# All scores of an image in one stage on eight 32x64 tiles, in a shifted-window attention block on one Trainium2 core

## What is computed

```python
h = ln(x) * g1 + b1                              # over the 64 channels
h = roll(h, (-4, -4)); win = partition(h, 8)     # 16 windows of 64 positions per image
q, k, v = split(win @ qkv_w + qkv_b)             # 4 heads of 16 channels
attn = q @ k.T * 16 ** -0.5 + bias(rpb) + mask   # 64 x 64 per window and head
out = softmax(attn) @ v @ proj_w + proj_b
x = x + unroll(out)
x = x + gelu(ln2(x) @ fc1_w + fc1_b) @ fc2_w + fc2_b
```

## Time and profile before

| what | value |
|---|---|
| time of the program, median of 3 | 505.39 us (505.28 to 506.8) |
| time of the profiled execution | 505.93 us |
| its span, first to last instruction | 504.1 us |
| busy: PE, PEld, DVE, ACT, POOL | 461.7, 351.5, 380.6, 294.8, 379.5 us |
| mean granted TensorE clock | 0.989 of full speed |

### The profile page before, as it was taken

One profiled execution on the slowest core, in us unless ns is written; L12 is line 12 of the kernel. 1 busy time (PEld: TensorE's weight loads), 2 busy tenths in 40 slices (PEclk: granted clock), 3 DMA queues, 4 the chain that ended last, 5 costly groups with the idle time before them and its releaser, 6 DMA issues.

```text
span 504.1 us, 21443 instructions
## 1 busy us (share of the span) xinstructions
PE 461.7 (92%) x9630; PEld 351.5 (70%) x9630; DVE 380.6 (75%) x549; ACT 294.8 (58%) x437; POOL 379.5 (75%) x376
## 2 busy tenths in 40 slices
PE   0766999999999999999999999996999999999995
PEld 0534877877877887887887877785566766667664
DVE  2765897898898888889889889793477667776652
ACT  1234567647656556566566665534666777667761
POOL 2658989979979979979979888840588888888830
PEclk9997999999999999999999999999899999999999
DMA  8201442411411411511110110100002311320333
GB/s 164 63 1 33 118 98 53 107 25 41 110 25 34 117 25 29 123 25 28 40 25 23 44 25 24 44 4 3 1 19 71 85 42 46 85 72 18 85 90 81
DMA packets 9986, 27.04 MB, mean 54 GB/s; under 512 B 3368, under 2 KB 3368, under 8 KB 7976
## 3 DMA queue, kind: packets, MB, share of 16 engines
q1 hardware_dynamic: 9896, 25.68, 21.4%
HBM read 9.15 MB, written 8.39 MB: 35 GB/s over the span
## 4 chain that ended last, share of the span: by engine, by line
PE 80%; ACT 9%; DMA 4%; DVE 3%; SPq 1%; issue 1%; ACTq 0%; DVEq 0%
PE work L686 27%; PE outs L686 18%; PE scores L686 13%; PE trans L686 8%; PE trans L782 6%; ACT kT L603 4%; PE scores L822 4%; PE work L701 3%; ACT qT L605 3%; DMA params<-in_params 2%; DMA kX<-kT 2%; PE outs L810 1%; SPq L277 1%; ACT probsT L638 1%; SPq L269 1%
## 5 line engine op out<-in xcount | busy, mean ns | idle before, releaser
L367 POOL TENSOR_TENSOR probs<-probs,negmax 128x1024 f32<-128x1024 f32 x64 | 124.4, 1945 | 27.0 <-DVE negmax L482 27.0
L333 POOL TENSOR_TENSOR stat_rstd<-stat_var,minus_half 128x8 f32<-128x8 f32 (+1 forms) x62 | 104.9, 1691 | 5.0
L476 DVE TENSOR_TENSOR probs<-scores,bias 128x1024 f32<-128x1024 f32 x64 | 78.1, 1220 | 27.3 <-PE scores L686 27.2
L638 ACT ACTIVATE probsT<-trans 128x1024 f32<-128x1024 f32 x64 | 65.5, 1023 | 27.0 <-PE trans L782 27.0
L338 POOL TENSOR_TENSOR xn<-x,stat_mean 128x256 f32<-128x256 f32 (+1 forms) x91 | 77.2, 866 | 4.1
L482 DVE TENSOR_REDUCE negmax<-probs 128x16 f32<-128x1024 f32 x64 | 78.1, 1220 | 2.2
L686 PEld LDWEIGHTS work<-params,probs 128*64 128x64 f32 x2048 | 62.2, 138 | 23.5 <-DVE x L570 20.5
L686 PE MATMUL scores<-kX,qT 32*64 32x128 f32 x2048 | 71.4, 276 | 7.4 <-DVE probs L476 4.6
L686 PEld LDWEIGHTS outs<-vX,probsT 128*64 128x64 f32 x2048 | 65.3, 138 | 13.7 <-issue 9.4
L782 PEld LDWEIGHTS trans<-ident,probs 128*128 128x128 f32 x512 | 56.2, 142 | 26.0 <-issue 13.0
L686 PE MATMUL outs<-vX,probsT 128*64 128x34 f32 x2048 | 72.1, 225 | 2.4 <-ACT probsT L638 1.4
(11 more groups left out here) (63 smaller groups left out, 656.2 us busy)
## 6 DMA issues: line engine op xcount, KB each, us to landing
kX<-kT SPq DMA_DIRECT2D x124, 64.0 KB, 2.0
x<-in_x SPq DMA_DIRECT2D x32, 224.0 KB
out<-x SPq DMA_DIRECT2D x28, 224.0 KB
x<-in_x SPq DMA_DIRECT2D x32, 32.0 KB
out<-x SPq DMA_DIRECT2D x28, 32.0 KB
out<-x SPq DMA_DIRECT2D x16, 56.0 KB
params<-in_params SPq DMA_DIRECT2D x1, 741.5 KB, 11.7
out<-x SPq DMA_DIRECT2D x16, 8.0 KB
```

What stands on the lines that cost most here:

```text
L333: nc.gpsimd.tensor_tensor(stat_rstd[:, cols], stat_var[:, cols], minus_half[:, cols], ALU.pow).then_inc(ln_rstd, pieces)
L367: nc.gpsimd.tensor_tensor(e, e, top, ALU.add).then_inc(shifted, 1)
L476: nc.vector.tensor_tensor(e[:, :].rearrange("q (u a m) -> q a u m", u=2, a=2), scores[:, :].rearrange("q (a u m) -> q a u m", a=2, u=2), b ...
L638: nc.scalar.activation(probsT[n % 2][:, :], trans[:, :], ACT.Exp)\
```

## The change

`score` now does a whole image (both pairs, k = 0 and 1) in one stage, on every odd step. The scores have four banks: the first pair uses the first two, the second pair the other two. The second pair's products go to the exchanged half of the partitions (`half = w ^ k`), so that eight tiles of 32 x 64 are addressed in turn. The mask has a third, turned block for it, and `weigh` reads the exchanged columns. The transposed probabilities no longer have banks of their own: `trans` is now the first pair's two banks. So `score(image)` also waits for the exponential of the pair before the last (`probsT_ready`), and `transpose_probs` also waits until DVE has read the first pair of the image scored last (`scores_taken`). Fills of even steps move behind the two transposes (on PE and on ACT), and the two halves of Y move from 4.5 and 6.5 to 6.5 and 8.5 (that is 0.5 of the next group).

```diff
-        tasks += [(4.5, "Y", 0), (6.5, "Y", 1)]
+        tasks += [(6.5, "Y", 0)]
...
+        if g >= 2:
+            found.append((STEPS * g + 0.5, "Y", g - 2, 1))
...
+    found.append((PAIRS + 0.5, "Y", GROUPS - 2, 1))
...
-        scores = psum("scores", 2)
-        trans = psum("trans", 2)
+        scores2 = psum("scores", 4)
+        scores = [scores2[:, 0:2 * BANK], scores2[:, 2 * BANK:4 * BANK]]
+        trans = scores[0]
...
-                dve.wait_ge(scores_ready, n + 1)
+                b = bias[:, 1:3, :] if k else bias[:, 0:1, :].to_broadcast([P, 2, BANK])
+                dve.wait_ge(scores_ready, n // 2 + 1)
...
-            def score(n):
-                image, k = divmod(n, 2)
+            def score(image):
...
-                if n:
-                    pe.wait_ge(scores_taken, n)
+                if image:
+                    pe.wait_ge(scores_taken, 2 * image)
+                if image > 1:
+                    pe.wait_ge(probsT_ready, 2 * image - 2)
                 for u in range(2):
                     for p in range(2):
-                        at = (2 * k + u) * P + p * N
-                        for w in range(2):
-                            for hh in range(2):
+                        for k in range(2):
+                            at = (2 * k + u) * P + p * N
+                            for w in range(2):
+                                half = w ^ k
+                                for hh in range(2):
...
+                                    out = scores[k][half * N:(half + 1) * N, hh * BANK + u * 256:][:, 0:256]\
...
-            def transpose_probs(n):
+            def transpose_probs(n, image):
+
                 pe.wait_ge(shifted, n + 1)
+                pe.wait_ge(scores_taken, 2 * image + 1)
...
-                            at = (u * HEADS + h) * P + w * N
+                            at = (u * HEADS + h) * P + (w ^ k) * N
...
             for n in range(PAIRS + TAIL):
-                if n + 1 < PAIRS:
-                    score(n + 1)
+                if n % 2 and n + 1 < PAIRS:
+                    score((n + 1) // 2)
                 if 0 <= n - PV < PAIRS:
                     weigh(n - PV)
-                for kind, of, i in tasks_at(n):
-                    fill(kind, of, i)
+                if n % 2:
+                    for kind, of, i in tasks_at(n):
+                        fill(kind, of, i)
                 if 0 <= n - TR < PAIRS:
-                    transpose_probs(n - TR)
+                    transpose_probs(n - TR, min((n + 1) // 2, PAIRS // 2 - 1))
                 if 0 <= n - OUT < PAIRS:
                     transpose_o(n - OUT)
+                if n % 2 == 0:
+                    for kind, of, i in tasks_at(n):
+                        fill(kind, of, i)
```

More of the change, by code:

```diff
@@ L58, in shift_masks @@
             out[wj % 2, :, v, wj // 2, :] = np.where(differ, NEG, 0.0)
-    return out.reshape(P, 2 * P)
+    straight = out.reshape(P, 2 * P)
+    turned = np.concatenate([straight[N:], straight[:N]])
+    return np.concatenate([straight[:, :P], turned], 1)
 TR, PV, OUT = 1, 2, 3
@@ L473, in bias_and_max @@
                 e = probs[n % 4]
-                dve.wait_ge(scores_ready, n + 1)
+                b = bias[:, 1:3, :] if k else bias[:, 0:1, :].to_broadcast([P, 2, BANK])
+                dve.wait_ge(scores_ready, n // 2 + 1)
                 nc.vector.tensor_tensor(
                     e[:, :].rearrange("q (u a m) -> q a u m", u=2, a=2),
-                    scores[:, :].rearrange("q (a u m) -> q a u m", a=2, u=2),
-                    bias[:, k:k + 2, :].rearrange("q u (a m) -> q a u m", a=2), ALU.add)\
+                    scores[k].rearrange("q (a u m) -> q a u m", a=2, u=2),
+                    b.rearrange("q u (a m) -> q a u m", a=2), ALU.add)\
                   .then_inc(scores_taken, 1)
@@ L637, in exp @@
                 act.wait_ge(trans_ready, n + 1)
[L638 removed]
+                nc.scalar.activation(probsT[n % 2][:, :], trans, ACT.Exp)\
                   .then_inc(probsT_ready, 1)
@@ L658, in _ @@
                     copy_oT(n - OUT)
+                if n % 2 == 0:
+                    for kind, of, i in tasks_at(n):
+                        take(kind, of, i)
                 for kind, of, i in tasks_at(n + 0.5):
@@ L739, in _ @@
             for t in range(3):
-                mm(scores[:, t:t + 1], wraw[:, t, :], shift[:, 0:1], stop=False)
-                mm(scores[:, t:t + 1], ident[:, :], bqkv_raw[:, t:t + 1], start=False)
+                mm(scores2[:, t:t + 1], wraw[:, t, :], shift[:, 0:1], stop=False)
+                mm(scores2[:, t:t + 1], ident[:, :], bqkv_raw[:, t:t + 1], start=False)
             for t in range(2):
-                mm(scores[:, 3 + t:4 + t], w1raw[0:C, t * P:(t + 1) * P], shift[0:C, 1:2], stop=False)
-                done = mm(scores[:, 3 + t:4 + t], ident[:, :], bf1_raw[:, t:t + 1], start=False)
+                mm(scores2[:, 3 + t:4 + t], w1raw[0:C, t * P:(t + 1) * P], shift[0:C, 1:2], stop=False)
+                done = mm(scores2[:, 3 + t:4 + t], ident[:, :], bf1_raw[:, t:t + 1], start=False)
             done.then_inc(biases_summed, 1)
@@ L765, in score @@
                 for u in range(2):
                     for p in range(2):
-                        at = (2 * k + u) * P + p * N
-                        for w in range(2):
-                            for hh in range(2):
-                                rows = slice(32 * (2 * w + hh), 32 * (2 * w + hh + 1))
-                                out = scores[w * N:(w + 1) * N, hh * BANK + u * 256:][:, 0:256]\
-                                    .rearrange("q (h p m) -> q p h m", h=2, p=2)[:, p]
-                                done = mm(out, qT[two][rows, at:at + N], kX[two][rows, :, at:at + N])
+                        for k in range(2):
[3 more added lines that the diff above has]
+                                for hh in range(2):
+                                    rows = slice(32 * (2 * w + hh), 32 * (2 * w + hh + 1))
+                                    out = scores[k][half * N:(half + 1) * N, hh * BANK + u * 256:][:, 0:256]\
+                                        .rearrange("q (h p m) -> q p h m", h=2, p=2)[:, p]
+                                    done = mm(out, qT[two][rows, at:at + N], kX[two][rows, :, at:at + N])
```

34 lines of the change are left out of this document (18 added, 16 removed).

## The result

The changed kernel took 500.4 us (median of 4 runs, 498.06 to 502.1), the kernel before beside it 505.75. The ratio is 0.9867, with a 95% interval from 0.9836 to 0.9899: faster, by 1.3%. The forecast was 489.0, 3.3% less than 505.75. So the sign was right, and less than half of the gain came. The profiled execution took 500.17 with a span of 498.4; the forecast for it was 489.5 and 487.7.

The account below looks back on a forecast made before the run. PE was taken to bound the attention; savings of 15.1 (six groups), 0.4 and 1.6 less 0.7 in the tail made 16.4 us, so 489.5 for the profiled execution and 489.0 as forecast, range 484 to 502 (0.8).

Parts of the forecast that it names:

- What bounds the kernel: In the attention, PE's queue: each microsecond leaving it is worth one, until DVE (0.87 of the period) or a wait takes over.
- The score stage: Both pairs' scores in one PE stage of 64 records over eight tiles: 1.09 us, instead of two stages of 1.03.
- The walk of two steps: Chain of waits through an odd and an even attention step: 8.90 to 9.05 us a cycle, 35.83 a group against 38.35.
- Next score stage: it waits for that step's exponential: After the even step's fills, the scores start 5.73 us (XT or no fill) or 5.81 (Y) after the odd step's transposes.
- Steps 3 to 9: 0.4 saved: First attention stretch: three cycles of 8.90 us make 26.7 against 27.11 before, so 0.4 saved.
- Steps 57 to 63: Last attention stretch: two cycles of 8.90 us and a third set by DVE's add, 25.9 against 27.48, so 1.6 saved.
- The tail: A half of Y (1.09 us) now stands in step 64.5, in a stretch with 0.46 of waiting: 0.7 lost.

Follow-up runs that it names:

- the other two edits: Changed kernel with the exponential in two halves, 491.4 us; changed kernel with the third group's rows loaded right behind the second's, 500.0 us; both together 490.9 us.
- the shifted stream: Changed kernel plus 16 small extra matmuls (64 PE instructions) at the start, while PE waits for parameters: 498.7 us, ratio 0.9853.
- the run with half the bytes: Changed kernel with all four key transfers of an image, each moving only the first half of its columns: 501.3 us, ratio 0.9887.
- the early rows: Changed kernel with the third group's rows loaded right behind the second's, not after the keys of step 1: 500.0 us, ratio 0.9851.

## Why the prediction was right and wrong, step by step

**What bounds the kernel.** Right in its sign: PE's queue. But "a microsecond that leaves PE's queue is worth a microsecond, until DVE or a wait takes over" held for 5.7 of the 24.8 us that left it; the rest went into waits, of which the prediction had foreseen 8.4 (24.8 less the 16.4 of its sum). One side remark of the prediction doesn't follow from its own sum: it says that half of the 3.9 us that the score stages save in a group goes into waits, but 2.5 of them are left (38.35 less 35.83), so it is a third. Nothing else used it.

**The score stage.** Right. 1.14 against 1.09, from rows of 64-row tiles. Had the exchanged tiles not run side by side, the stage would have been 1.90. The rule of the Trainium skill (TensorE: Matmul & The Clock Gate, the mechanism of packing) that weight loads overlap with running matmuls only on other row groups is, taken as the prediction took it, not what these runs show: 1.14 against 1.90 is the gain of running two tiles on each row group. Nor does its floor of about 25 ns from one matmul to the next (section on the gap above 53.3 ns) hold for these tiles: 64 records in 1.14 are 18 ns each.

**The walk of two steps.** Right where nothing else waits: 8.97 to 9.02 measured, 8.90 to 9.05 forecast, with 0.35 for 0.34 of waiting for the exponential ahead of `weigh`, and 0.98 for 1.0 where no fill covers.

**The step that failed: "Next score stage: it waits for that step's exponential", with no word on the keys.** My walk followed PE, ACT and DVE, and left out SP. The stage also waits for `kX_loaded`, and that chain (key copy, four issues of 0.6 us on SP, landing 2.0 us) needs 5.2 us from QK, and the shorter cycle leaves 5.7, so a landing stretched by more than 0.5 us shows. The prediction had put this wait at nothing, without a word, although shows one of 0.29 us before the change. Two issues in place of four brought the ratio from 0.9867 or 0.9901 to 0.9728, which is 7 to 9 us (give or take 3, by the intervals), and on top of the other two edits 8 and 6.5; in the traces the attention became 6.0 and 7.2 shorter. So this chain, with what hangs on it, is more than half of the 11 us that were missing. Part of it may be the breaks below rather than the wait itself: the shifted stream, which still waited 5.2 us for keys, also had an attention 3 to 4 us shorter. That two transfers beat four fits what the Trainium skill (DMA: Bandwidth & Descriptors, rules for kernel authors) says of partition halves, to use one transfer of 128 partitions instead; that their number counts and not their bytes is what the run with half the bytes shows, and that the issuing is what they save is read from SP's queue, 1.1 us for 2.4.

**"Steps 3 to 9: 0.4 saved."** Wrong by 2.5; the stretch took 2.1 more than before. 1.8 of it is the cycle from step 5 to 7: I took no wait of DVE for its rows, although it had waited 1.06 there in the kernel before (at 59.20), without harm. It waits 1.89 now, `weigh` waits 0.48 for DVE behind that, and the transposes 1.39 for its add. The prediction had named that last wait and called it covered. Another 0.6 is a break in V. The 1.0 that two score stages wait for the exponential, where the first group has no Y to fill, isn't part of the miss: the walk had it inside its 8.90.

**Steps 57 to 63.** 1.1 more than forecast. The score stage at 323.71 waits 1.26, for the keys at last where the walk has 1.0 for the exponential, and a QK stage at 307.15 takes 1.65 instead of 1.09. With two transfers the stretch took 26.1, as good as the forecast.

**The tail.** Right: 0.7 lost.

**Not foreseen and only partly explained:** the breaks inside stages, 1.3, 0.6 and 0.4 us in the changed kernel, and two QK stages of 1.4 and 1.65 instead of 1.09. The shift of the stream shows that they belong to places in it, and the run with fewer key transfers that traffic has a part in their length; it doesn't remove them all (QK takes 1.61 there at 292.41, a score stage 1.53 at 181.63). That PE waits there for a block of instructions that comes by DMA as the keys do (the instruction queue moved 76 packets in all) fits both, and is argued, not shown. What they cost on the whole was not measured apart: the breaks in the rows sum up to 2.3 and 1.6 us, and the shifted kernel, with 0.9 before a V and 0.29 in a Y, is 3 to 4 us shorter in the attention, but by its time only within the intervals faster.

## What to carry to other kernels

When a change shortens the period of a bound engine, list every semaphore that its stages wait for, and walk each of those chains through, the issuing queue's time for each transfer too: a transfer hidden with 1 us to spare is the next bound. Small matmuls on different tiles, rows shared or not, are worth putting into one stage; the length of such a stage was near the rounds' streaming plus 0.2 us (1.14 and 1.90, for 1.03 and 1.85 by that rule). Where one engine's long instruction stands between two stages of the bound engine, cutting it in half at a bank's boundary (here 64 more instructions on ACT) can bring as much as the change that exposed it (7 to 9 us here, for 5 to 7). And compare kernels stretch by stretch: the early rows looked worthless in the total, but took 1.1 to 3.3 us out of one stretch and, with four key transfers, gave them back in another.

## What was unexpected of the hardware

- Eight 32 x 64 tiles, two on each row group, ran 32 float32 products of 128 columns in 1.14 us; the same products on four tiles took 1.90.
- Four transfers from SP cost 0.6 us each to issue (median), whether of 64 or of 32 KB, and two of 128 KB, 0.5 us each, carried the same keys and made the kernel 6.5 to 9 us shorter.
- PE can stop in the middle of a stage for up to 1.3 us with no semaphore to wait for, at the same record in two executions. With the stream shifted by 64 instructions, one such stop moved by 32 records, and the longest was gone.
- After a wait of 2.34 us the granted clock was 0.57 on average for 4 us, and the weighing took 1.93 us instead of 1.13.
